# A two-layer transformer kernel: rows of C read back from DRAM instead of multiplied out, and expert blocks with standing gate and up weights

## The reference, cut to what matters

```python
# state-space layer, for each batch: N = 16 states, D = 512 channels, T = 512 tokens
xz = einsum('btd,rd->btr', x, W_xproj)          # 128 + 16 + 16 rows
B_mat, C_mat = xz[..., 128:144], xz[..., 144:160]
h = dA_t * h + Bu_t                             # one scan over t for each state and channel
y = sum(h * C_t[:, None, :], axis=-1)           # every state has its own row of C over t
# expert, for routed tokens (7 routed experts, top 2; one shared)
h = silu(x @ wg) * (x @ wu) / 8                 # wg, wu: 512 x 256
out = h @ wd                                    # wd: 256 x 512
```

## Time and profile before

| | |
|---|---|
| median of 3 runs | 2076.64 us (2075.48 to 2079.7) |
| the profiled execution's own time | 2075.01 us |
| its span | 2073.3 us |
| TensorE matmul busy | 1868.7 us (90%) |
| VectorE busy | 1355.5 us (65%) |
| ScalarE busy | 999.4 us (48%) |
| GpSimd busy | 799.6 us (39%) |
| granted TensorE clock, mean | 0.942 |

### The profile page before, as it was taken

The page is one execution under the profiler, slowest core; times in us unless marked ns, Lnnn a source line. Parts: engine busy times, 40 slices in busy tenths (PEclk is TensorE's granted clock), DMA queues, the critical chain, the costliest instruction groups (busy, mean ns, idle before and its releaser), DMA issues. The chain is left out here.

```text
span 2073.3 us, 27455 instructions
## 1 busy us (share of the span) xinstructions
PE 1868.7 (90%) x9242; PEld 1224.6 (59%) x9242; DVE 1355.5 (65%) x2164; ACT 999.4 (48%) x1739; POOL 799.6 (39%) x1065
## 2 busy tenths in 40 slices
PE   7978665899999899999999899999999899999795
PEld 3446444695448555596447655587447665588342
DVE  5766699575563699576654599676754599667311
ACT  1412685363432698363332599264342499365131
POOL 1146177552220177471220167481310157472301
PEclk9989755999999999999999999999999999999898
DMA  6337200000213076210113167210022157310493
GB/s 256 107 101 234 102 0 20 2 2 1 102 46 122 22 256 225 92 37 21 62 71 109 39 224 250 106 42 21 36 97 92 56 185 262 132 42 22 189 374 106
DMA packets 56505, 221.06 MB, mean 107 GB/s; under 512 B 6320, under 2 KB 6320, under 8 KB 48560
## 3 DMA queue, kind: packets, MB, share of 16 engines
q1 hardware_dynamic: 47216, 195.19, 26.9%
q0 software_dynamic: 5120, 16.78, 2.5%
q10 hardware_dynamic: 4032, 7.34, 1.0%
HBM read 179.70 MB, written 39.58 MB: 106 GB/s over the span
## 5 line engine op out<-in xcount | busy, mean ns | idle before, releaser
L2055 POOL TENSOR_TENSOR Y<-Y,HC 128x1024 f32<-128x1024 f32 x116 | 273.7, 2360 | 175.0 <-DVE HC L1424 174.3
L1413 DVE TENSOR_TENSOR_SCAN HS<-DA,ps 128x1024 f32<-128x1024 f32 x128 | 292.4, 2285 | 24.2 <-PE ps L782 13.5
L1795 ACT ACTIVATE DA<-DL,AB,AN 128x511 f32<-128x511 f32 x256 | 193.9, 807 | 14.7 <-DVE HS L1413 13.5
L1036 PE MATMUL ps<-ring,XBT 128*128 128x512 f32 x384 | 188.5, 597 | 0.2 <-ACT XBT L1474 0.2
L558 PE MATMUL ps<-ring,XNT 128*128 128x512 f32 x384 | 178.4, 619 | 9.0 <-PEq L2090 9.0
L1912 ACT ACTIVATE PD<-ps,NMX 128x128 f32<-128x128 f32 (+3 forms) x256 | 134.8, 529 | 99.3 <-DVE NMX L1557 96.7
L1557 DVE TENSOR_REDUCE NMX<-ps 128x1 f32<-128x128 f32 (+3 forms) x256 | 124.5, 488 | 63.7 <-PE ps L874 63.3
L892 PE MATMUL ps<-V,PTD 128*128 128x33 f32 x1280 | 164.1, 261 | 0.0
L892 PEld LDWEIGHTS ps<-V,PTD 128*128 128x128 f32 x1280 | 162.5, 192 | 0.4 <-ACT PTD L914 0.4
L690 PE MATMUL ps<-XNH,tern 128*128 128x512 f32 x352 | 139.6, 397 | 9.2 <-DVE tern L1313 5.5
L1424 DVE TENSOR_TENSOR HC<-HS,ps 128x1024 f32<-128x1024 f32 x120 | 143.3, 1197 | 0.0
(11 more groups left out here) (254 smaller groups left out, 4020.1 us busy)
## 6 DMA issues: line engine op xcount, KB each, us to landing
ring<-experts_dram SPq DMA_DIRECT2D x48, 1024.0 KB, 5.3
tern<-tern_q SPq DMA_DIRECT2D x33, 768.0 KB, 4.3
ring<-experts_dram SPq DMA_DIRECT2D x48, 512.0 KB, 5.5
RAW<-tern_dram SPq DMA_DIRECT2D x22, 768.0 KB, 4.8
XB<-xg SPq DMA_DIRECT2D x42, 256.0 KB, 3.7
yg<-YB SPq DMA_DIRECT2D x42, 256.0 KB, 4.9
ring<-wqkv_dram SPq DMA_DIRECT2D x3, 3072.0 KB, 12.1
tern_q<-tern SPq DMA_DIRECT2D x11, 768.0 KB, 7.0
```

What stands on the lines that cost most here:

```text
L1036: last = pe.matmul(ps[:, g_bank(b)], XBT[:, b % 2, k], weights(b)[:, k * C:(k + 1) * C], start=(k == 0), stop=(k == NK - 1), skip_group_ch ...
L1413: v.tensor_tensor_scan(HS[:, q].rearrange("p j t -> p (j t)"), DA[:, q].rearrange("p j t -> p (j t)"), ps[:, 2 * q:2 * q + 2].rearrange("p ...
L1795: s.activation(DA[:, u % 2, jj, 1:T], DL[:, j, 1:T], ACT.Exp, scale=AN[:, j * NS + n:j * NS + n + 1], bias=AB[:, j * NS + n:j * NS + n + 1 ...
L2055: p.tensor_tensor(y, y, HC[:, q], ALU.add).then_inc(c_y, 1)
```

## The change

Each state's row of C is no longer multiplied out. RB holds 32 rows (B, then C) instead of 96; SyncE stores the 16 rows of C to a DRAM tensor `c_rows`, waits for it, and reads each row back with a transfer that repeats it on all 128 partitions, into one of three SBUF buffers CR. `v_C_out` reads CR. `p_split` and `pe_C_row` are gone, and `packb` loses the 0/1 matrix. In `step` without experts SyncE loads all rows before the shared expert's weights.

In the expert blocks the gate and up weights now stand and the tokens stream: 16 products of 128x128 weights with 128 token columns. The result has the hidden units on the partitions, so HB goes straight into the down product; `pe_block_t` and `block_ht` are gone.

```diff
+        def store_c(sp):
+            sp.wait_ge(c_rb, 1)
+            sp.dma_start(c_rows, RB[NS:2 * NS]).then_inc(c_stored, 16)
+            sp.wait_ge(c_stored, 16)
+            for n in range(3):
+                load_c(sp, n)
+
+        def load_c(sp, n):
+            if n >= 3:
+                sp.wait_ge(c_hc, 2 * (n - 2))
+            sp.dma_start(CR[n % 3][:], c_rows[n:n + 1, :].to_broadcast([P, T])).then_inc(row_loaded[n % 3], 16)
...
         def v_C_out(v, u):
             n, q = divmod(u, 2)
-            v.wait_ge(c_rowC, n + 1)
+            v.wait_ge(row_loaded[n % 3], 16 * (n // 3 + 1))
             v.wait_ge(c_scan, u + 1)
             if u >= 4:
                 v.wait_ge(c_y, u - 3)
             dst = Y[:, 2 * q:2 * q + 2] if n == 0 else HC[:, q]
-            v.tensor_tensor(dst, HS[:, q], ps[:, 4:5, :].to_broadcast([P, 2, T]), ALU.mult).then_inc(c_hc, 1)
+            v.tensor_tensor(dst, HS[:, q],
+                            CR[n % 3][:].rearrange("p (o t) -> p o t", o=1).to_broadcast([P, 2, T]), ALU.mult).then_inc(c_hc, 1)
...
-            for k in range(k0, k1):
-                last = pe.matmul(ps[:, g_bank(b)], XBT[:, b % 2, k], weights(b)[:, k * C:(k + 1) * C],
-                                 start=(k == 0), stop=(k == NK - 1), skip_group_check=True)
+            for m in range(k0, k1):
+                for k in range(NK):
+                    last = pe.matmul(ps[:, g_bank(b), tile(m)], weights(b)[:, k * C + m * P:k * C + (m + 1) * P],
+                                     XBT[:, b % 2, k], start=(k == 0), stop=(k == NK - 1), skip_group_check=True)
...
-        def pe_block_t(pe, b):
-            pe.wait_ge(m_h, b + 1)
-            for m in range(2):
-                last = pe.transpose(ps[:, g_bank(b), tile(m)], HB[:, b % 2, tile(m)], ident)
-            last.then_inc(m_t, 1)
-
         def pe_block_down(pe, b):
-            pe.wait_ge(m_ht, b + 1)
+            pe.wait_ge(m_h, b + 1)
...
-                last = pe.matmul(ps[:, d_bank(b)], HBT[:, b % 2, m], weights(b)[:, c:c + C],
+                last = pe.matmul(ps[:, d_bank(b)], HB[:, b % 2, tile(m)], weights(b)[:, c:c + C],
...
         def p_C(p, experts):
-            p_split(p, experts)
...
                         for n in range(NB + 2):
+                            if 1 <= n < NS - 2:
+                                load_c(sp, n + 2)
                             if n + 2 < NB:
```

More of the change, by code:

```diff
@@ L57 @@
 _at = 0
-for _name, _n in (("wo", NK * C), ("wx", NK * RANK), ("wbc", NK * 96), ("wdt", C), ("wkvd", NK * P),
+for _name, _n in (("wo", NK * C), ("wx", NK * RANK), ("wbc", NK * 2 * NS), ("wdt", C), ("wkvd", NK * P),
                   ("wqd", NK * P), ("wq", C), ("wk", C // 2), ("wv", C), ("wkr", NK * C // 2),
@@ L67 @@
 NLATE = PACK["ident"][0]
-NPACKB = NS * P + 4 * P
+NPACKB = 4 * P
 NU = NH * NT
@@ L154, in build @@
     region("packb", -(-NPACKB * 2 // 32) * 32)
+    region("rows", 4 * KB)
     region("ring", 3 * ESIZE * 4)
@@ L262, in build @@
     HC = at("HC", [P, 2, 2, T], F32, "tern")
-    R1 = at("R1", [96, T], F32, "tern", 8 * KB)
-    BCS = at("BCS", [96, T], BF16, "tern", 10 * KB)
+    CR = [at(f"CR{n}", [P, T], F32, *(("rows", 2 * n * KB) if n < 2 else ("tern", 8 * KB))) for n in range(3)]
     BT = at("BT", [P, NT, 32], F32, "tern", 11 * KB)
-    RB = at("RB", [96, T], F32, "tern", 16 * KB)
+    RB = at("RB", [2 * NS, T], F32, "tern", 16 * KB)
     UT = at("UT", [P, NT, C], F32, "v1")
@@ L312, in build @@
     sin_d = cst("sind").rearrange("p (i s d) -> p i s d", i=NT, s=2)
-    sel = packb[0:96, 0:NS * P].rearrange("p (r n) -> p r n", n=P)
-    identb, mask_q, lower, onesb = (packb[:, NS * P + n * P:NS * P + (n + 1) * P] for n in range(4))
+    identb, mask_q, lower, onesb = (packb[:, n * P:(n + 1) * P] for n in range(4))
     wqkv = ring[:, 0:2, :].rearrange("p s n -> p (s n)").rearrange("p (k n) -> p k n", k=NK)
@@ L414, in build @@
         c_bc = sem("c_bc")
-        c_split = sem("c_split")
+        c_stored = sem("c_stored")
         c_z = sem("c_z")
@@ L430, in build @@
         c_b = sem("c_b")
-        c_rowC = sem("c_rowC")
+        row_loaded = [sem(f"row_loaded{n}") for n in range(3)]
         c_da = sem("c_da")
@@ L746, in pe_C_prep @@
             for k in range(NK):
-                last = pe.matmul(ps[0:96, 7], wbc[:, k], XNT[:, k], start=(k == 0), stop=(k == NK - 1))
+                last = pe.matmul(ps[0:2 * NS, 7], wbc[:, k], XNT[:, k], start=(k == 0), stop=(k == NK - 1))
             last.then_inc(c_bc, 1)
@@ L758, in pe_C_prep @@
                     last.then_inc(c_bt, 1)
[L760 to L767, removed]
         def ub(n, i):
@@ L787, in pe_C_out @@
             if experts:
-                pe.wait_ge(m_ht, NB)
+                pe.wait_ge(m_h, NB)
                 pe_E_down(pe, 2)
@@ L1389, in v_C_prep @@
             delta(3)
[L1391 to L1405, removed]
         def v_C_scan(v, u):
@@ L1783, in s_C_prep @@
                     s.wait_ge(c_bc, 1)
-                    s.copy(RB[:], ps[0:96, 7]).then_inc(c_rb, 1)
+                    s.copy(RB[:], ps[0:2 * NS, 7]).then_inc(c_rb, 1)
         def s_C_decay(s, u):
@@ L1838, in s_scan @@
                 s_C_decay(s, 2 * m)
-                if done:
-                    block_ht(s, s.copy, n - 2)
                 ub_part(2)
@@ L1848, in s_scan @@
             if experts:
-                block_ht(s, s.copy, NB - 1)
                 block_y(s, s.copy, NB - 1)
@@ L2260, in _ @@
                     else:
+                        store_c(sp)
+                        for n in range(3, NS):
+                            load_c(sp, n)
                         sp.dma_start(ring[:, 2], exp_in[0]).then_inc(next_loaded, 16)
@@ L2428 @@
     packb = np.zeros((P, NPACKB), np.float32)
-    for n in range(NS):
-        packb[[NS + n, 32 + NS + n, 64 + NS + n], n * P:(n + 1) * P] = 1.0
-    t0 = NS * P
+    t0 = 0
     packb[:, t0:t0 + P] = np.eye(P)
@@ L2465 @@
     out = nc.dram_tensor("out_dram", (B * T, C), F32, kind="ExternalOutput").ap()
-    build(nc, *aps, tern_q, xg, yg, out)
+    c_rows = nc.dram_tensor("c_rows", (NS, T), F32, kind="Internal").ap()
+    build(nc, *aps, tern_q, xg, yg, c_rows, out)
     r = run_bass_kernel_spmd(nc, [{k + "_dram": v for k, v in arrays.items()}], core_ids=[0])
```

28 lines of the change are left out of this document (6 added, 22 removed).

## The result

The changed kernel takes 2108.05 us (median of 5 runs, 2107.59 to 2108.66) against 2075.8 for the kernel before, measured beside it (5 runs). The ratio is 1.0149, 95% interval 1.0138 to 1.016: 32 us slower by the medians and 31 by the ratio, where 26.6 were forecast. The profiled execution took 2107.59 us, span 2105.9.

What follows compares the result with a forecast made beforehand. VectorE was taken to bound the scans, TensorE `finish`. The terms 3.8 + 25.7 - 2.9 = 26.6 us on 2075.0 gave 2101.6, and 2103 with the median's 1.6; range 2091 to 2115.

Steps and rivals of the forecast that it cites:

- Bound by VectorE in the scans, by TensorE in `finish`: Scans run at VectorE's pace, 7.63 us per two-unit iteration with blocks; `finish` at TensorE's, 5.81 us a block.
- Contention at 24 products, nothing at the others: Scans: GpSimd and VectorE's two-SBUF-input product hold each other up; all but the first 0.2 us waits; 25.7 us lost.
- The product's own duration: Scans: VectorE's product with two SBUF inputs takes 1.225 us against 1.195, adding 3.8 us; lower bound 0.
- The split at nothing: Ahead of each scan: removing GpSimd's split instructions costed at nothing; 4.4 us gained at most.
- The row through DRAM at nothing: Scans: stores and loads of C's rows land before use, hidden behind more than one iteration; costed at nothing.
- `finish` at -2.9: `finish`: 0.10 us less per block, 1.4 in all, and 1.5 at its end; bounds 1.5 and 3.5.
- no contention for a plain product: Rival, scans: VectorE's product is never held up by GpSimd; 2074 to 2078; chance 0.11 for no change, 0.04 for faster.
- Contention for the whole instruction: Rival, scans: VectorE must hold the read path from its start, so ordinary units lose time too; 2114 us, chance 0.10.
- Weight loads in the open: Rival, expert blocks: the 16 up products cannot hide their weight loads and take 0.38 us each; 2205 us, chance 0.03.
- Rows late: Rival, scans: products wait for C's rows from DRAM if landing takes over 7 us; 2130 to 2155 us, chance 0.02.

Runs made afterwards that it cites:

- the dose: Four further GpSimd scalings a scan into a buffer nothing reads: changed kernel 2123.36 us, ratio 1.0222; kernel before 2075.53 us, ratio 0.9993.
- the blocks alone: The kernel before with only the new expert blocks, the row of C by split and product as before: 2073.93 us, ratio 0.9986.
- row-only kernel: The changed kernel with the old expert blocks (tokens standing, HB transposed): 2113.32 us, ratio 1.0175.
- the respaced one: The changed kernel with GpSimd's XNT scalings before its first add and the XNT adds behind products 0 and 1: 2079.37 us, ratio 1.0015.
- the one with both cures: The changed kernel with GpSimd's XNT scalings and adds moved to the scan's head and the last state's products reading PSUM: 2077.61 us, ratio 1.0007.
- the one with halved adds: The changed kernel with each GpSimd add of line 2004 split in two of 128x512: 2118.0 us, ratio 1.0201.

## Why the prediction was right, point by point

**Bound by VectorE in the scans, by TensorE in `finish`: shown.** In the scans a longer product costs its own lengthening: the dose makes the products 12.9 us longer in all and the kernel 15 us slower, and the blocks alone, which change TensorE's work there, change no scan.

**Contention at 24 products, nothing at the others: right, and slightly under-sized.** Forecast 25.7 us, measured 28.1. The step that gives the difference is "so the first 0.2 us of an instruction run meanwhile": for this product it is 0.12, so the loss is 1.30 instead of 1.24 behind a scaling and 2.07 instead of 2.04 behind an XNT add in batch 0, and 0.74 and 1.54 to 1.74 with blocks, where 0.66 and 1.46 stood. The 1.74 is the second XNT add's: it starts 0.06 us behind the start of a product and takes 3.37, the first one starts 0.25 behind and takes 3.18. The number of held products and who holds whom came out as worked, from two rows of other lines; the place did in 23 of 24, and in batch 0 the last hold fell one unit later, on product 25. In the working itself, 284.25 + 2.35 is 286.60, not 286.58; nothing hangs on it.

**The product's own duration: wrong.** "0.03 x 32 x 4 = 3.8 us" took the repeated-tensor product of line 1228 as the model. The median went from 1.195 to 1.199, 0.5 us in all. The nearest row was of another operand pattern; the lower bound was right.

**The scans' ends: missing.** The prediction counted six units a scan and did not look at its end. Products 30 and 31 lie back to back, and the last add, on which the output transposes wait, is held by 0.9 us: X comes 3.0 us later in all. Reading the last row from PSUM gave 2.1 of them back in the traces. Of the rest, 0.3 us in batches 1 and 2 and 0.1 in batch 3 stand with the new blocks alone.

**The split at nothing: right.** Line 1349 is at 0.75 throughout, and from the start of the preparation to the second scan it is 0.11 us longer, not shorter.

**The row through DRAM at nothing: right** as to lateness; the first product comes at 251.19, long behind the loads.

**`finish` at -2.9: right in kind.** The blocks-only ratio gives -2.9 (-5.0 to -0.8). A block is 0.08 shorter, forecast 0.10. The lower bound of 1.5 was mis-worked: with 0.23 us a product a block would be 0.02 longer, not the same, which leaves 1.2.

**Outside the two stages** 2.9 us came on that no term had: 1.3 ahead of the first scan's preparation, which starts anywhere from 231.5 to 237.1 us in the runs here, whatever the kernel, and 1.6 between the scans, most of it in one place. There, in the attention ahead of the scan of batch 3, VectorE falls back 1.5 us. The windows of that stretch (busy times of TensorE, its weight loads, VectorE, ScalarE and GpSimd, then the granted clock, DMA share, GB/s), before and then after:

```profile
1512.00:1516.00 4.00, 3.88 (x16) 1.45 (x14) 0.00 (x0) 1.57 (x3) 1.78 (x3) 0.57 0.99 415
1516.00:1520.00 4.00, 4.00 (x30) 1.99 (x28) 3.05 (x5) 2.43 (x3) 0.00 (x0) 1.00 0.05 16
```

```profile
1534.00:1538.00 4.00, 3.35 (x26) 1.85 (x24) 0.00 (x0) 3.94 (x5) 0.89 (x2) 0.91 0.90 352
1538.00:1542.00 4.00, 4.00 (x16) 1.31 (x15) 0.00 (x0) 1.51 (x2) 1.57 (x3) 0.50 0.96 396
1542.00:1546.00 4.00, 4.00 (x26) 2.10 (x22) 2.43 (x5) 1.14 (x2) 0.00 (x0) 0.74 0.04 17
```

The granted clock drops to half in both, 1.2 of 2.4 GHz. By the means of these windows it stays there for some 3.4 us before and some 6.8 after, and TensorE is busy all but throughout. The same step of 1.5 us stands at the same place, with the same longer stretch at half clock, in batch 2 of the profiles of the row-only kernel, the one without a second GpSimd instruction, the respaced one and the one with both cures, and in batches 2 and 3 of the dosed changed kernel. The other profiles have the short stretch there and no step: all three of kernels that multiply the row out, the one where ScalarE copies the row, but also the one with the last row from PSUM and the one with halved adds. So the time goes with the clock; what keeps the clock down longer, the row through DRAM or chance, is open.

**The sum: near by terms that partly cancel.** From 26.6 forecast to 32.6 us of span: the product's duration 3.4 less, the held products 2.4 more, the scans' ends 3.0, the way to the second scans 0.4, outside the two stages 2.9, and `finish` 0.8 less of a gain (2.1 instead of 2.9 from the last scan to the end). The mechanism carried 28.1 of them. That the forecast of 2103 lies only 5 us from 2108 owes something to an overestimate that covered a missing term.

Of the rivals, "no contention for a plain product" fell with the first long product. "Contention for the whole instruction" fell with the 104 ordinary products at 1.20. Weight loads in the open: 3.57 us for 32 records, none. Rows late: no such wait.

## What to carry to other kernels

Before an operand of a VectorE instruction is moved from PSUM to SBUF, lay GpSimd's timeline beside it: if both its inputs are then in SBUF, a GpSimd instruction that is still running when it starts costs its whole remainder (all but 0.12 us of it in these runs, for adds and scalings that read SBUF), and one VectorE instruction back to back with another does the same to GpSimd. What counts is the place, so the first cure is to move GpSimd's extra work to where VectorE reads one of its inputs from PSUM, as the scans do here; cutting the adds into pieces did not help. Such a hold is booked as busy time, so compare a line's median with its maximum and mean, not its waits.

## What the hardware showed unexpectedly

- A product of two SBUF tensors, one repeated over two blocks, runs in 1.199 us undisturbed, against 1.195 with the repeated one in PSUM: the move itself costs 0.5 us over 128 products.
- A held product keeps a head start of 0.12 us, the same behind a whole add, behind a half, and in the ordinary unit of the halved kernel.
- The one that comes first pays nothing: the product ahead of a held scaling took 1.20 us, while the scaling went from 1.57 to 2.56.
- Two adds of 128x512 on GpSimd last 2.49 us where one of 128x1024 lasts 2.35.
